# Third feed-forward stage: a tile's transposes and the lane's next projections as one phase

## What is computed

```python
def _layer(x, wqkv, qs, ksc, wo, lg, lb, w1, b1, w2, b2):
    h = shift_token(x)
    q, k, v = jnp.split(h @ wqkv, 3, axis=-1)
    q, k, v = (to_heads(q), to_heads(k), to_heads(v))
    q = l2norm(q) * qs
    k = l2norm(k) * ksc
    q, k = rotary_xpos(q, k)
    o = local_attention(q, k, v)
    x = x + o @ wo
    h = shift_token(x)
    ...
    x = x + (a * jax.nn.gelu(g, approximate=False)) @ w2 + b2
```

## Time and profile before

| | |
|---|---|
| median of three runs | 6159.2 us (6155.87 to 6160.15) |
| profiled execution | 6145.7 us |
| its span, first to last instruction | 6144.4 us |
| mean granted TensorE clock | 0.734 |
| busy TensorE, VectorE, ScalarE, POOL | 66%, 55%, 32%, 17% |
| the stage of the change | from about 4079 to 5610 us of the span |

### The profile page before, as it was taken

How to read it: one execution, slowest core, us unless ns; L and a number is a source line. 1 busy time by engine, 2 the same in 40 slices (tenths; PEclk the granted TensorE clock), 3 DMA queues, 4 the chain that set the end, 5 groups by cost and what they waited for, 6 DMA issues and landing times.

```text
span 6144.4 us, 101520 instructions
## 1 busy us (share of the span) xinstructions
PE 4030.2 (66%) x42812; PEld 3038.8 (49%) x42812; DVE 3358.9 (55%) x8341; ACT 1942.5 (32%) x4236; POOL 1071.5 (17%) x784
## 2 busy tenths in 40 slices
PE   4655555565877878764555756567666777666298
PEld 3544444453655555553444645444444454445277
DVE  7677777615455555556345454555665555655333
ACT  2222322222333333321224232324444444443122
POOL 4040404041111011113400000011111111110434
PEclk6555555587888988976666666668877888778599
DMA  9000000041000000001200000000000000000155
GB/s 245 23 1 1 1 1 2 30 125 47 1 1 1 1 1 1 1 19 26 55 2 1 2 1 2 1 2 1 1 1 1 1 1 1 1 1 1 65 156 142
DMA packets 140744, 148.60 MB, mean 24 GB/s; under 512 B 7792, under 2 KB 127986, under 8 KB 139776
## 3 DMA queue, kind: packets, MB, share of 16 engines
q1 hardware_dynamic: 118880, 124.05, 7.1%
q0 software_dynamic: 21408, 18.05, 1.7%
HBM read 83.22 MB, written 59.76 MB: 23 GB/s over the span
## 4 chain that ended last, share of the span: by engine, by line
PE 42%; DVE 36%; ACT 11%; issue 5%; POOL 2%; DMA 2%; another core or an unknown queue 1%; SPq 0%; DVEq 0%; POOLq 0%; ACTq 0%
ACT work L3174 3%; PE banks_lane L422 3%; DVE weights L1207 3%; DVE work L1207 2%; PE banks_lane L3611 2%; PE banks_lane L1830 2%; PE banks_lane L3016 2%; PE banks_lane L3060 2%; PE banks_lane L933 1%; DVE weights L3267 1%; ACT work L1924 1%; PE banks_lane L3095 1%; PE banks_lane L793 1%; DVE work L2737 1%; PE banks_lane L3082 1%
## 5 line engine op out<-in xcount | busy, mean ns | idle before, releaser
L422 PE MATMUL banks_lane<-constants,work 128*128 128x128 f32 x936 | 195.9, 358 | 452.3 <-DVE work L408 195.8
L402 POOL TENSOR_TENSOR weights<-weights,constants 128x4 f32<-128x4 f32 x80 | 82.7, 1034 | 1964.8 <-DVE weights L397 1964.8
L422 PE MATMUL banks_lane<-constants,weights 128*128 128x128 f32 x628 | 133.2, 356 | 426.4 <-DVE weights L408 135.1
L422 PEld LDWEIGHTS banks_lane<-constants,work 128*128 128x128 f32 x936 | 149.6, 185 | 527.9 <-DVE work L408 185.6
L3174 ACT ACTIVATE work<-banks_lane,weights 128x192 f32<-128x192 f32 (+1 forms) x512 | 248.6, 499 | 245.6 <-DVE weights L3271 245.6
L422 PEld LDWEIGHTS banks_lane<-constants,weights 128*128 128x128 f32 x628 | 97.2, 183 | 457.4 <-issue 171.4
L3279 POOL TENSOR_TENSOR weights<-weights,constants 128x16 f32<-128x16 f32 x64 | 185.5, 2898 | 530.7 <-DVE weights L3187 530.7
L402 POOL TENSOR_TENSOR work<-work,constants 128x4 f32<-128x4 f32 x72 | 73.4, 1020 | 1173.1 <-DVE work L397 1173.1
L3095 PE MATMUL banks_lane<-constants,work 128*128 128x128 f32 x896 | 149.6, 316 | 120.6 <-DVE work L3259 70.8
L1977 DVE TENSOR_REDUCE work<-banks_lane 128x2 f32<-128x512 f32 x256 | 158.8, 683 | 67.6 <-PE banks_lane L1844 67.2
L1207 DVE SCALAR_TENSOR_TENSOR weights<-weights 128x512 f32<-128x512 f32 x220 | 188.9, 859 | 4.8
(11 more groups left out here) (820 smaller groups left out, 11409.8 us busy)
## 6 DMA issues: line engine op xcount, KB each, us to landing
work<-experts_dram_l_ffn SPq DMA_DIRECT2D x39, 964.0 KB
room_l_ffn<-work SPq DMA_DIRECT2D x30, 1188.0 KB, 15.2
work<-experts_dram_l_ffn SPq DMA_DIRECT2D x23, 512.0 KB
weights<-weights_dram SPq DMA_DIRECT2D x1, 4833.5 KB, 14.6
work<-room_l_ffn SPq DMA_DIRECT2D x36, 132.0 KB
weights<-weights_dram SPq DMA_DIRECT2D x1, 4112.0 KB, 12.5
weights<-room_l_ffn SPq DMA_DIRECT2D x26, 132.0 KB
weights<-weights_dram SPq DMA_DIRECT2D x1, 3378.0 KB, 11.2
```

The source lines that it names most:

```text
L402: pool.tensor_tensor(n.rstd, n.rstd, c("neghalf", cols=(0, n.rstd.shape[1])), ALU.pow).then_inc(*u.pool.step(name))
L422: done = pe.transpose(bank[0:rows, t * P:(t + 1) * P], block, c("ident"))
```

## The change

In all four programs of `L2Ffn`, the yield after `rotate{t}` goes for the first three tiles. So the transposes of tile t and the projections of tile t + 1 of the same lane are issued as one phase, named `project{t+1}`, and only the last tile's transposes keep a phase of their own. No instruction and no wait is changed.

```diff
@@ pe
                 made.then_inc(*u.pe.step(f"flipped{t}_{n}"))
-            yield f"rotate{t}"
+            if t == TILES - 1:
+                yield "rotate"
```

## The result

The changed kernel takes 6102.3 us in the median of four runs (6091.7 to 6112.0), the kernel before 6159.7 us (6155.9 to 6163.7, four runs). The ratio is 0.9902, with a 95% interval of 0.9888 to 0.9916: 57 us or 1.0% faster. The forecast was 6101 us.

A forecast was written before the change was run, and what follows sets the result against it. No engine is full, so handovers bound the kernel, with VectorE waiting at steps from lane A to B. A pass saves 17.9 - 10.2 - 0.5 = 7.2 us, eight passes 58 us: median 6101 us, range 6085 to 6131 without rivals.

The forecast's parts named there:

- The order and the removed waits: Projection part: VectorE's order becomes A0 A1 B0 A2 B1 A3 B2 B3, removing four A-to-B waits, 17.9 us a pass.
- The handovers at A1 and B3: Head and tail of a pass's projection part: VectorE waits 4.36 us plus 0.22 to 1.02 at each, 10.2 us together.
- The five tiles between: B0, A2, B1, A3, B2: TensorE takes about 6 us a tile within VectorE's 6.34; waits 0.5 us a pass.
- rival 1: Projection part: clock stays low, TensorE becomes the bound; a pass saves about 1.8 us, 6145 us; chance 7%.
- The sum: Third feed-forward stage: a pass saves 17.9 - 10.2 - 0.5 = 7.2 us, eight passes 58 us.
- the forecast's own range: Whole kernel, main case without the rivals: 32 to 71 us saved, some 5 us either way, 6085 to 6131 us.
- What follows the projections: Attention behind the projections in each pass: scores queued behind P(B3) are covered by VectorE's 7 us; costs nothing.
- Rival 3: Attention behind the projections: loses its clock, up to 64 us slower, 6220 us; chance 4%.
- Median against profile: Whole kernel: median of three runs stands 13.5 us above the profiled execution, so 6088 us becomes 6101 us.

The follow-up runs named there:

- e1: Only tile 0's transposes share a phase with the next projections (one merge), otherwise as the kernel before; ratio to before 1.000.
- e2: Transposes of tiles 0 and 1 merged with the next projections, tile 2's not (two merges), otherwise as the kernel before; ratio to before 0.993.
- e3: Changed kernel, but lane B has its shift and first projections in one phase and an empty phase ahead of its last transposes; 5985.0 us, ratio to before 0.973.
- e9: e3 again, unchanged, with more rounds on another chip; 6001.5 us, ratio to before 0.9737.
- e10: e3 with the third product of every tile's projections issued three times; 5989.5 us, ratio to before 0.9730.
- e5: Changed kernel with three extra products behind lane A's last transposes, keeping TensorE busy; one execution, stage 1433.9 us against the changed kernel's 1450.4.
- e6: Changed kernel with the third product of every tile's projections issued twice; one execution, stage 1437.5 us against the changed kernel's 1450.4.

## Why the prediction was right

*The order and the removed waits: right.* The four waits of 3.46 + 1.02 us a pass are gone; e1 and e2 show the same rule with other orders, and e3 with none left.

*The handovers at A1 and B3: right in place and kind, 0.15 us small.* I had 4.36 us, measured 4.51. The term that was mis-sized is the time from the projection's issue to the square: I took 1.95 us from B0, whose product followed directly on transposes; after a pause it is 2.11 us (4173.54 to 4175.65), which the kernel before shows too at the stage's very first product (4094.04 to 4096.15). The second square's wait was 1.02 us in nearly all, where I had taken 0.74 in the mean (5.1 less 4.36). Together 11.0 us a pass instead of 10.2.

*The five tiles between: right in effect, wrong in the reason.* I expected TensorE to swing between the levels, about 6 us a tile, and 0.5 us of waits. There were none, and in the middle of the first pass the granted clock was 1.00 throughout (4146.73 to 4165.44), with TensorE busy for 11.80 us in three tiles, 3.9 each. That is the first pass alone. In each of the other seven the clock fell once inside the middle tiles, for 3.41 us. TensorE's timeline of the second pass, and the stretches before and in the fall:

```profile
4339.91 0.66 PE L3023 MATMUL banks_lane<-constants,work 128*128 128x128 f32 x4 [1.63 <-DVE work L3203]
4341.24 4.38 PE L3016 MATMUL banks_lane<-weights,work 128*128 128x512 f32 x6 [0.68 <-ACT work L3130]
...
4337.57:4340.98 3.41, 1.36 (x9) 0.78 (x7) 3.27 (x8) 1.51 (x4) 0.49 (x1) 1.00 0.00 0
4340.98:4344.39 3.41, 3.15 (x4) 1.51 (x5) 3.34 (x9) 0.81 (x2) 2.90 (x1) 0.50 0.00 0
```

Before it fell, TensorE had the end of its products, eight transposes and a pause: busy 1.36 of 3.41 us. The next projections then took 4.38 us where a tile's took 2.84 at 4335.00, and VectorE still did not wait, since a tile at the high clock (4.74 us by the forecast's sum) leaves TensorE about 1.5 us of VectorE's 6.24. So the rule that transposes don't count as busy, from the Trainium skill's page "TensorE: Matmul & The Clock Gate", section on the PE-mode transpose, is not refuted here: the fall after transposes and a pause agrees with it, though most tiles of the same pattern passed without a fall. What it did not bring about is rival 1, a clock that never rises: the high level came back each time, and the slack of a tile covered the fall.

*The sum: 7.2 us a pass forecast.* The eight projection parts give 552.2 - 493.9 = 58.3 us, 7.3 a pass. By waits alone it is 55.3 us. The other 3 us come with them: where no wait stands, two reduces take 1.27 us instead of 2 x 0.69, and the next tile's first begins 0.09 us before line 3205 has ended (4165.37 + 0.16 against 4165.44); 16 handovers fewer by 0.2 us are 3.2 us. The handovers, 0.8 us a pass larger than forecast, and the middle and these overlaps, together 0.9 smaller, cancelled. The ends of the forecast's own range are 2 and 1 us off by its terms: 6159 less 71 less 5 is 6083, and 6159 less 32 and 5 more is 6132.

*What follows the projections.* I had put it at nothing. The seven rests gave 3.6 us: two of them took 116.6 us, and the first four were about as long as before (118.9 to 119.2 against 118.6 to 119.0). Rival 3, the attention losing its clock, had the sign wrong: in every experiment the seven rests were shorter than before, by 2.8 us (e9) to 27.5 us (e10).

*Median against profile.* The offset of 13.5 us that I carried over from the profiled execution to the median was not a property of the kernel: the changed kernel's profiled execution (6108.8 us) stands 6.5 us above its median. With a spread of 25 us in one untouched stage the forecast of the median within 1 us is in part luck.

## What to carry to other kernels

Where two lanes take turns on in-order engines, write down each engine's order over a few steps and ask, for each handover, what stands on the producer's queue ahead of the consumer's next input. The gain comes from issuing the consumer's next input while the consumer is still at work on the present one; merging phases in one place only moves the wait, and here a third of the change alone lengthened its own part. Read the stage's own stretch in the trace: whole times of single runs moved by 20 us and more for reasons outside the change.

## What had not been expected

- A stretch of the same instructions in the same order takes 113.3 to 120.4 us, and the second attention stage 1318.6 to 1345.0 us in profiles of kernels in which it is the same; at 1320.5 us the granted clock was 0.88, at 1340.7 it was 0.86. The mean clock alone does not set the length: e5's first rest took 117.1 us at 0.85, the changed kernel's 118.9 us at 0.86. This spread moves the whole time as much as a third of the change.
- More work for TensorE shortened its stage three times: e5 by 16.5 us and e6 by 12.9 against the changed kernel, e10 by 27 against e9. Over the stage the granted clock was higher in all three (0.85 and 0.87 against 0.84, 0.93 against 0.86). In the rests alone it was clearly so in e10 (0.90 against 0.84), hardly in e6 and e5 (0.865 and 0.859 against 0.856), so that the clock is what shortened e5's rests by 7.1 us is not shown. How much of it reaches the whole time is open.
- Two merges gave nearly twice what their waits account for (41 against 23 us). The rests were 15.4 us shorter; what in the order puts the late passes' rests at 115 us and not at 119 was not looked into further.
